# Local attention layers of a fused network on one Trainium2 core: the turn of the keys moves to another place in each slot

## What is computed

```python
def attn_layer(x, Wqkv, qs, ksc, Wo):            # 16 heads of 64
    q, k, v = split heads of x @ Wqkv
    q = l2norm(q) * qs;  k = l2norm(k) * ksc
    q = q * cos * scale + rotate_half(q) * sin * scale
    k = k * cos / scale + rotate_half(k) * sin / scale
    # windows of 32 queries see their own and the previous window: 64 keys
    sim = einsum('bhwie,bhwje->bhwij', bq, bk2) * 8, masked
    out = einsum('bhwij,bhwje->bhwie', softmax(sim), bv2)
    return out @ Wo
for i in range(6):
    x = attn_layer(shift_tokens(x), Wqkv[i], q_scale[i], k_scale[i], Wo[i]) + x
    x = ffn_layer(shift_tokens(x), ln_g[i], ln_b[i], W1[i], b1[i], W2[i], b2[i]) + x
```

## Time and profile before

| | |
|---|---|
| median of 3 runs | 1283.91 us (1281.17 to 1284.33) |
| span of the profiled execution | 1280.5 us |
| TensorE matmuls busy | 1215.7 us (95%) |
| VectorE busy | 986.7 us (77%) |
| ScalarE busy | 938.3 us (73%) |
| GpSimd busy | 785.7 us (61%) |
| DMA queue of the program | 79.03 MB, 22.4% of 16 engines |

### The profile page before, as it was taken

One profiled execution on the slowest core, in us unless ns is written; L12 is line 12 of the kernel. 1 busy time (PEld: TensorE's weight loads), 2 busy tenths in 40 slices (PEclk: granted clock), 3 DMA queues, 4 the chain that ended last, 5 costly groups with the idle time before them and its releaser, 6 DMA issues.

```text
span 1280.5 us, 44796 instructions
## 1 busy us (share of the span) xinstructions
PE 1215.7 (95%) x17900; PEld 871.3 (68%) x17900; DVE 986.7 (77%) x2513; ACT 938.3 (73%) x2310; POOL 785.7 (61%) x805
## 2 busy tenths in 40 slices
PE   7999988999999999999999999999999999999996
PEld 5777745676767667767777677767677877777553
DVE  4666677888888788888888888888888656778677
ACT  6777775677777677777777777777777758788891
POOL 3444447878878787788777877778776102635000
PEclk9999998999999999999999999999999989999989
DMA  5000032222224322342225222422232001202000
GB/s 213 1 2 1 2 116 73 70 61 58 61 62 110 96 60 63 82 127 57 63 59 149 58 63 64 128 79 61 62 86 54 2 15 74 83 32 92 1 1 17
DMA packets 71743, 81.89 MB, mean 64 GB/s; under 512 B 15456, under 2 KB 63584, under 8 KB 71024
## 3 DMA queue, kind: packets, MB, share of 16 engines
q1 hardware_dynamic: 71536, 79.03, 22.4%
HBM read 31.22 MB, written 0.56 MB: 25 GB/s over the span
## 4 chain that ended last, share of the span: by engine, by line
PE 46%; DVE 19%; ACT 18%; issue 11%; POOL 5%; DMA 1%; SPq 0%; DVEq 0%; ACTq 0%; POOLq 0%
PE banks L823 3%; PE banks L808 3%; PE banks L391 2%; DVE arena L2862 2%; DVE arena L2861 2%; DVE small L2870 2%; PE banks L1143 2%; PE banks L1137 2%; PE banks L420 2%; DVE arena L2883 2%; DVE arena L2863 2%; DVE small L2871 2%; PE banks L1165 2%; PE banks L405 2%; PE banks L751 2%
## 5 line engine op out<-in xcount | busy, mean ns | idle before, releaser
L3998 POOL TENSOR_TENSOR arena<-arena,small 128x512 f32<-128x512 f32 x93 | 97.1, 1044 | 136.2 <-DVE small L2885 136.2
L1906 ACT ACTIVATE arena<-banks 128x512 f32<-128x512 f32 x94 | 56.1, 597 | 139.5 <-PE banks L759 139.3
L2861 DVE TENSOR_TENSOR arena<-banks,rotary 128x512 f32<-128x512 f32 x192 | 131.6, 685 | 22.7 <-ACT arena L1876 9.2
L3973 POOL TENSOR_TENSOR arena<-arena 128x512 f32<-128x512 f32 x96 | 122.7, 1278 | 26.3 <-DVE arena L2863 26.2
L808 PE MATMUL banks<-arena 64*64 64x32 f32 x5824 | 107.3, 221 | 15.5 <-issue 8.3
L3978 POOL TENSOR_TENSOR arena<-arena 128x512 f32<-128x512 f32 x95 | 121.4, 1278 | 0.2 <-DVE arena L2863 0.2
L607 POOL TENSOR_TENSOR arena<-arena,small 128x512 f32<-128x512 f32 x64 | 66.6, 1041 | 89.0 <-DVE small L534 89.0
L808 PEld LDWEIGHTS banks<-arena 64*64 64x64 f32 x5824 | 95.8, 135 | 27.0 <-ACT arena L1928 11.4
L3985 POOL TENSOR_TENSOR arena<-arena,small 128x512 f32<-128x512 f32 x95 | 99.5, 1047 | 5.6 <-ACT small L1916 5.6
L722 PE MATMUL banks<-slot,z 128*128 128x512 f32 x192 | 100.1, 603 | 1.3 <-DVE arena L2863 0.9
L3992 POOL TENSOR_TENSOR arena<-arena,small 128x512 f32<-128x512 f32 x95 | 99.2, 1044 | 0.0
(11 more groups left out here) (403 smaller groups left out, 3368.8 us busy)
## 6 DMA issues: line engine op xcount, KB each, us to landing
arena<-arena SPq DMA_DIRECT2D x576, 64.0 KB, 2.1
slot<-in_pack_dram SPq DMA_DIRECT2D x28, 339.5 KB, 3.4
arena<-arena SPq DMA_DIRECT2D x288, 32.0 KB, 1.9
slot<-in_pack_dram SPq DMA_DIRECT2D x2, 2713.5 KB, 9.2
slot<-in_pack_dram SPq DMA_DIRECT2D x1, 2693.5 KB
slot<-in_pack_dram SPq DMA_DIRECT2D x1, 2316.5 KB
arena<-gate_store SPq DMA_DIRECT2D x8, 256.0 KB, 3.9
slot<-in_pack_dram SPq DMA_DIRECT2D x4, 337.0 KB, 3.6
```

The costliest lines, as they stand in the source:

```text
L2861: e.tensor_tensor(rot, made, cos, ALU.mult)
L3973: e.tensor_tensor(m.rot_q[u % ROTS], m.rot_q[u % ROTS], m.sin_q[u % 2], ALU.add).then_inc(s["q_added"], 1)
```

## The change

In each slot of the local layers, `pe_local` calls `pe_turn_key` for unit s-2 between the turn of the weights and the scores, where it was called behind the feed-forward matmuls of the slot.

```diff
--- before.py
+++ after.py
@@ -855,6 +855,8 @@
             pe_centre(e, s, m, ended(slot, CENTRE))
         if live(slot - VALUE):
             pe_turn_weights(e, s, m, slot - VALUE)
+        if live(slot - TURN):
+            pe_turn_key(e, s, m, slot - TURN)
         if live(slot - SCORE):
             pe_scores(e, s, m, slot - SCORE)
         if live(slot - VALUE):
@@ -867,8 +869,6 @@
             pe_last_hidden(e, s, m, ended(slot, LAST), min(slot - SCORE + 1, UNITS))
         if ended(slot, GATE2) is not None:
             pe_last_gate(e, s, m, ended(slot, GATE2))
-        if live(slot - TURN):
-            pe_turn_key(e, s, m, slot - TURN)
         if ended(slot, MERGE) is not None:
             pe_ffn_out(e, s, m, ended(slot, MERGE), min(slot - SCORE + 1, UNITS))
```

## The result

The changed kernel takes 1292.94 us (median of 4 runs, 1291.56 to 1298.85); the kernel before took 1283.41 us beside it. The ratio is 1.0093, with a 95% interval of 1.0065 to 1.0122. The prediction was 1281.4 us with a range up to 1286.5, so it was wrong in its direction and outside its range. The profiled execution has a span of 1289.8 us, 9.3 us more than before. It took 1291.56 us, so only 1.8 us lie around a span; the 3.4 us put there for the kernel before also hold the distance of its profiled execution from its median.

A forecast was written before the change was run, and what follows sets the result against it. A round between VectorE and ScalarE was taken to pace the local layers. Undisturbed groups 0, catching up after stalls -1.8 and first slots -0.7 us made -2.5 us, from 1283.9 to 1281.4 us; range 1275 to 1286.5 us.

The forecast's parts named there:

- The round: Local layers: VectorE and ScalarE, waiting on each other, pace each four-slot group; undisturbed groups 33.1 to 33.4 us; chance 0.65.
- rival (a): Local layers: TensorE paces after all, so all relieved waits come back, 12 us, giving 1272 us; chance 0.16.
- TensorE's reserve: TensorE waits for the round in four places a group: 0.30 us before L808, 0.33, 0.09 and 0.09 us before L751.
- The relieved waits: Earlier key copy and cover for L1928 help TensorE catch up after stalls, 1.8 us, and first slots, 0.7 us.
- The new wait at L1897: Ahead of the scores, the moved turn waits for the query copy, replacing waiting before L808; cost 0.
- The stalls as a given: L808's 12 idle times without a releaser, 8.3 us, vary by two or three of 0.7 us; 4 us either way.
- (b): The delayed block reaches the round at L2918, then L2871: 0.43 us in 23 groups, 10 us slower, 1294 us; chance 0.12.
- Rival (c): Eight transposes in a row at L792 and L759 lower TensorE's clock in six layers: 10 us, 1294 us; chance 0.03.
- Rival (d): ScalarE reaches the key copy only behind L1928, so the move frees nothing: 1284 us; chance within the round's 0.65.

The follow-up runs named there:

- e9: Kernel before with two needless 128x128 products right ahead of the scores, behind their waits; 1296.5 us, ratio 1.0127.
- e6: Changed kernel with two needless 128x128 products between the scores and the weighted sum in each slot; 1310.9 us, ratio 1.0237.
- e16: Changed kernel with the scores' waits and the k_rotated wait ahead of the turn of the weights, normalised-weights wait on its first matmul; 1272.5 us, ratio 0.9924.
- e17: Kernel before with the scores' waits moved ahead of the turn of the weights, whose first matmul carries the normalised-weights wait; 1278.3 us, ratio 0.9977.
- e15: Changed kernel with the scores' waits ahead of the turn of the keys, whose first matmul carries the q_kept wait; 1275.6 us, ratio 0.9956.
- e5: Kernel before with the q_kept wait moved from the turn of the keys onto the scores' first matmul; 1282.5 us, ratio 1.0000.
- e13: Kernel before with the q_kept wait moved to the last event instruction ahead of the scores; 1289.2 us, ratio 1.0050.
- e12: Changed kernel with the two waits of the turn of the keys swapped, so q_kept rides on its first matmul; 1288.9 us, ratio 1.0055.
- e8: Kernel before with the turn of the keys between scores and weighted sum, and 32 tiny products shifting packet boundaries; 1278.0 us, ratio 0.9976.
- e14: Repeat run of the kernel before with the turn of the keys moved between scores and weighted sum; 1276.3 us, ratio 0.9962.
- e3: Changed kernel with 32 tiny products added in the second slot, shifting packet boundaries by 128 instructions; 1296.3 us, ratio 1.0106.

## Why the prediction was wrong

1. **The round.** Right as far as the length of the undisturbed groups goes: 33.0 to 33.1 us against 33.15, forecast 33.1 to 33.4, so rival (a), with 32.5 us or less, is out. TensorE's reserve was real but smaller than the places counted for it (0.7 us in e9), and all but gone in the changed order (e6). That VectorE and ScalarE alone pace the changed kernel is therefore not shown; e6 speaks against it.
2. **The relieved waits.** Right. L808 stopped waiting for L1928, and L751 waits more around the gelu copies. Take the fit's 0.68 x 15.8 + 0.46 x 10.3 = 15.5 us off the 12.3 us by which the stage grew, and 3.2 us of gain are left where 2.5 were forecast. It is no more than a plausibility: the fit misses by as much. With the waits out of the way in both orders there is more to go by: e16, in the changed order, is 5.8 us faster than e17, in before's, though their intervals just touch and e16 also has the wait for k_rotated moved. So the move seems to have a gain of its own, which the new wait buried.
3. **The new wait at L1897: the step that failed.** The prediction asked what the turn's wait does to the matmuls, found that "what it waits here it no longer waits there", and put it at 0. For the matmuls that holds: 2.4 us idle before L759, most of it in one slot. But TensorE's matmuls were not the only ones to stand there. The sequencer, which in before had run past this point, stood at it in 84 of 91 slots, and packets of instructions that fell due there started only behind it. Price: e15 against the changed kernel, 17.4 us between the medians; some of that is a gain the moved waits bring in before's order too (e17, 0.23%, 3 us).
4. **The stalls as a given.** "Two or three stalls of 0.7 us more or fewer, 4 us either way" treated the 8.3 us of the earlier trace rows as noise that the order doesn't touch. They grew to 23.2 us in 18 places, and with them the falls of the clock. All 12 were there to be placed in the program; they would have stood at the same count modulo 256, and the question what moves ahead of that count would have followed.
5. **Rivals.** The sign of (b) came true, and its place too, but by another mechanism: no mask waited for the scores and the multiply L2861 waited for L1876 about as before (10.5 us against 9.2), while the hidden multiply L2918 did come late, 17.3 us against 3.2, behind stalls and not by the turn's 0.43 us. Rival (c), the clock, was half right: the level fell, but behind idle time and not behind transposes; in e15 the eight transposes in a row stand as in the changed kernel and the level does not fall once in the stage. Rival (d) is out.

## What to carry to other kernels

An idle time that nothing in the profile ends is a cost with a cause: number the engine's instructions and see whether the places share a count modulo 256. Where a run of short instructions without a pause is as long as a packet (here 256), put the wait that may take long on a matmul, with the event instructions of that place ahead of it, by the order of the waits in the source. Here such a wait left 9.3 us (e5) and 9.5 us (e15) of stalls in the weighted sum; on an event instruction it left 14.1 us (e13), and on a matmul with event instructions still to come behind it 23.1 us (e12). A move that changes no duration and no wait of a matmul can still cost 1%, if it puts a wait for a late copy ahead of such a run.

## What was unexpected of the hardware

- TensorE gets its program in packets of 256 instructions. A late one lets it go on 2.4 to 2.7 us behind the packet's start (medians of the 19 kernels: 2.36 to 2.69), of which the transfer itself is 1.1 to 1.3 us.
- A packet that falls due while the sequencer stands ahead of the scores starts 1.05 to 1.14 us behind the last event instruction there (medians by kernel; 1.24 to 1.37 in e8, e14 and e16). Inside the sequencer nothing can be seen; the rule is what the traces and e15 show, not an explanation. Some packets came later than that: the one at 311.12 was 1.66 us behind, and no run says why.
- Of the 13 falls to 1.2 GHz in the stages of before, the changed kernel and e3 (2, 6 and 5), 11 start within 1.6 us behind a stall of 1.4 us or more; the fit prices one of 3.4 us at 1.6 us.
